# An attention-weight kernel of a recommender: the set-up stage reordered (loads, warm-up matmuls, biases, layout, split of the bank reads)

## Chip, cores and metric

The kernel runs on one core of a Trainium2 chip. The metric is the device time of one execution in microseconds, the median of several.

## The reference

For each of B = 2048 rows with one candidate vector `c` (32 numbers) and N = 200 goods vectors `g` (32 numbers each):

```python
outer = jnp.einsum('bi,bnj->bnij', candidate_ad, goods).reshape(Bs, Ns, Ks * Ks)
k_b = jnp.broadcast_to(candidate_ad[:, None, :], (Bs, Ns, Ks))
h1 = jnp.concatenate((k_b, goods, outer), axis=-1)
act = jax.nn.sigmoid(h1 @ W1 + b1)          # 36 hidden numbers
weight = act @ W2 + b2
out = jnp.sum(goods * weight, axis=1)
```

Because `outer` is a product of `c` and `g`, `h1 @ W1` is `g` times a 32x36 matrix that depends on the row alone (W1's goods part plus the outer part contracted with `c`), plus a bias that depends on the row alone (`c @ W1_cand + b1`). The kernel builds these per-row matrices and biases once and then streams the goods.

## The kernel before, in words

Four rows of B lie side by side on the 128 partitions (32 each) and make a unit; there are 512 units, and 8 units make a pair (64 pairs).

**Set-up.** The candidates (`cand`, 1 MB: 128 partitions of 8 KB), W1's outer part (`w1`, named `w_outer` in the trace) and small constants are loaded. In nine steps (`step(i)`, L229) TensorE makes, for four hidden numbers at a time, the outer part of the weights: one PSUM bank of 512 columns for each `x` in 0..3, from row group `x` of `cand` and of `w1`. Step 0 makes the last four hidden numbers (h = 32..35, the left-over weights), steps 1 to 8 the 32 main ones. Even steps write the four banks of `z_ps`, odd steps `x_ps`, `w_ps` and the two `s_ps`. Each bank is read out with W1's goods part added: ACT takes x = 0 and 2 (L350), DVE x = 1 and 3 (L377), 18 banks each. A step from 2 on waits for the reads of the step two before. The main banks go to `wm`. The left-over banks go to `wxd` with the four hidden numbers innermost, so that ACT and DVE write with a step of four elements (16 bytes). POOL first zeroes `wx` (L182) and then copies `wxd` into it (L189, `lay_out`, four copies of 32x256 elements for 8 pairs; `lay_out(0)` and `lay_out(1)` in the set-up, the six others in the loop, each behind the split of pair q = 0, 8, ... 40).

Between step 0 and step 1 TensorE makes the biases: L238 (32 columns of weights against 512 columns of `cand`, four column groups, all from row group 0) into `x_ps`, and L245 into `w_ps`. DVE reads both (L380, L383), and step 1 waits for these reads, since it writes the same banks.

**Main loop.** For each pair p, TensorE multiplies goods by `wm` (`products`, L265) and by `wx` (`products_x`, L281), ACT takes the sigmoid (L363, L359), TensorE sums over the hidden numbers (L301, `row_sums`), DVE keeps the sum (`whole`, L390), POOL splits it into three bf16 parts (L201 to L210, `top`, `rest`, `mid`, `stack`), TensorE spreads these over partitions (L317, `spread`, three pairs later), and DVE multiplies with the goods and sums (L398). SP issues the loads of the goods (L168) once `w1` and the constants have landed, into seven slots. `cand`, `candu` and `w1` lie in the memory that `act` takes later. The order on each queue is that of the program; semaphores tie the engines together. An f32 matmul is two records in the trace, so a bank of step 0 to 8 is 8 records.

Of the kernel before, what the change touches and what calls it, by code (L numbers as in the profile page):

```python
# [6 lines left out]
BF16 = mybir.dt.bfloat16  # L7
ALU = mybir.AluOpType
# [14 lines left out]
STORE = 16  # L23
WX_CHUNK = 8
WX_AHEAD = 2
RUN = 16
POOLED_ORDER = (0, 4, 2, 6)

# [14 lines left out]
def build(nc, goods_t, cand_r, cand_u, w1_outer, small, pick, out_t):  # L43
    with ExitStack() as ctx:
        def sb(name, shape, dt=F32):
            return ctx.enter_context(nc.sbuf_tensor(name, shape, dt))
# [6 lines left out]

        goods = sb("goods", [P, G_SLOTS, PAIR_U, N])
        wm = sb("wm", [P, UNITS // RUN, HM, RUN])
        wxd = sb("wxd", [P, UNITS // 2, 2, HX])
        warm = sb("warm", [P, 1])
        wx = sb("wx", [P, UNITS // 2, 3, 16])
        act = sb("act", [P, A_SLOTS, 4, 2 * N])
        actx = sb("actx", [P, A_SLOTS, N])  # L60
# [45 lines left out]

        def wxd_units(x):

            return wxd[:, :, :, x].rearrange("j (p c) s -> j p s c", c=4)

        def wb_units(x):
            return wb_bank(0, x).rearrange("j (p s c) -> j p s c", s=2, c=4)

        def wm_units(h):
            return wm[:, :, h, :]
# [5 lines left out]
        cand_loaded = sem("cand_loaded")  # L121
# [20 lines left out]

        block = ctx.enter_context(nc.Block())

        def kept(i, x):

            return 2 * i + x // 2 + 1

        KEPT_ALL = 2 * (T_MAIN + 1)

        def laid_out(k):

# [1 line left out]

        @block.sync
        def _(sp):
            sp.dma_start(cand[:, :, :], cand_r[:, :, :]).then_inc(cand_loaded, 16)
            sp.dma_start(candu[:, :], cand_u[:, :]).then_inc(candu_loaded, 16)

            sp.wait_ge(w1_loaded, 16)  # L160
            sp.wait_ge(consts_loaded, 16)
            for p in range(PAIRS):
                for j, v in enumerate(POOLED_ORDER):
                    if p >= G_SLOTS:

# [12 lines left out]
            sp.wait_ge(out_stored, 16 * (PAIRS // STORE))  # L178

        @block.gpsimd  # L180
        def _(pool):
            nc.gpsimd.memset(wx[:, :, :, :], 0.0).then_inc(wx_step, 1)  # L182

            def lay_out(k):

                of = slice(4 * WX_CHUNK * k, 4 * WX_CHUNK * (k + 1))
                for r in range(4):
                    rows = slice(32 * r, 32 * r + 32)
                    nc.gpsimd.tensor_copy(wx[rows, of, 0::2, HX * r:HX * r + HX], wxd[rows, of, :, :]).then_inc(wx_step, 1)  # L189
                    pool.wait_ge(wx_step, 4 * k + r + 2)  # L190

            pool.wait_ge(wx_step, 1)

            pool.wait_ge(wb_kept[0], kept(0, 2))
            pool.wait_ge(wb_kept[1], kept(0, 3))
            for k in range(WX_AHEAD):
                lay_out(k)
            pool.wait_ge(consts_loaded, 16)
            for q in range(PAIRS):
                pool.wait_ge(w_kept, q + 1)  # L200
                nc.gpsimd.tensor_scalar(top[:, :], whole[:, q % 2, :], m1, None, ALU.mult).then_inc(part_step, 1)  # L201
                pool.wait_ge(part_step, 4 * q + 1)
                nc.gpsimd.tensor_tensor(rest[:, :], whole[:, q % 2, :], top[:, :], ALU.subtract).then_inc(part_step, 1)  # L203
                pool.wait_ge(part_step, 4 * q + 2)
                nc.gpsimd.tensor_scalar(mid[:, :], rest[:, :], m2, None, ALU.mult).then_inc(part_step, 1)  # L205
                pool.wait_ge(part_step, 4 * q + 3)
                if q >= 2:

                    pool.wait_ge(s_done, 2 * (q - 1))
                nc.gpsimd.tensor_tensor(stack[:, q % 2, :], rest[:, :], mid[:, :], ALU.subtract).then_inc(part_step, 1)  # L210
                k = q // WX_CHUNK + WX_AHEAD
                if q % WX_CHUNK == 0 and k < PAIRS // WX_CHUNK:
                    pool.wait_ge(part_step, 4 * q + 4)
                    lay_out(k)

        @block.tensor
        def _(pe):
            pe.wait_ge(w1_loaded, 16)
            pe.wait_ge(cand_loaded, 16)

            def step(i):
                for x in range(4):
                    if i == 1 and x < 2:

                        pe.wait_ge(bias_kept, x + 1)
                    if i >= 2:
                        pe.wait_ge(wb_kept[x % 2], kept(i - 2, x))
                    for c in range(4):
                        last = nc.tensor.matmul(wb_bank(i, x)[32 * c:32 * c + 32, :],  # L229
                                                w1[32 * x:32 * x + 32, STEPS[i], :],  # L230
                                                cand[32 * x:32 * x + 32, c, :], start=True, stop=True)
# [39 lines left out]

            def products_x(p, s):
                if s == 0:
                    if p % WX_CHUNK == 0:
                        pe.wait_ge(wx_step, laid_out(p // WX_CHUNK))
                    if p >= 1:

                        pe.wait_ge(act_done, 4 * p)
                for c in range(4):
                    left = wx[:, 4 * p + c, s:s + 2, :].rearrange("p b m -> p (b m)")  # L280
                    last = nc.tensor.matmul(x_bank(p)[32 * c:32 * c + 32, 0:N], left,  # L281
                                            goods[:, p % G_SLOTS, 4 * s + c, :], start=s == 0, stop=s == 1)
                if s == 1:
                    last.then_inc(x_done, 1)
# [52 lines left out]
        def _(sc):  # L337
# [4 lines left out]
            sc.wait_ge(warm_set, 1)  # L342
            nc.scalar.activation(warm[:, :], warm[:, :], ACT.Sigmoid)
            sc.wait_ge(consts_loaded, 16)
            for i, t in enumerate(STEPS):
                for x in (0, 2):
                    sc.wait_ge(wb_made, 4 * i + x + 1)
                    h = 4 * t + x
                    out, src = (wxd_units(x), wb_units(x)) if i == 0 else (wm_units(h), wb_runs(i, x))
                    nc.scalar.activation(out, src, ACT.Identity, bias=w1g[:, h:h + 1]).then_inc(wb_kept[0], 1)  # L350
            sc.wait_ge(bias_kept, 2)
            for p in range(PAIRS):
                if p >= A_SLOTS:
# [14 lines left out]
        @block.vector  # L368
        def _(dve):
            nc.vector.memset(warm[:, :], 0.0).then_inc(warm_set, 1)  # L370
            dve.wait_ge(consts_loaded, 16)
            for i, t in enumerate(STEPS):
                for x in (1, 3):
                    dve.wait_ge(wb_made, 4 * i + x + 1)
                    h = 4 * t + x
                    out, src = (wxd_units(x), wb_units(x)) if i == 0 else (wm_units(h), wb_runs(i, x))
                    nc.vector.tensor_scalar(out, src, w1g[:, h:h + 1], None, ALU.add).then_inc(wb_kept[1], 1)  # L377
# [96 lines left out]
```

## Time and profile before

| | |
|---|---|
| Median of 3 runs | 292.26 us (291.7 to 293.32) |
| The profiled execution's own time | 290.82 us |
| Its span, first to last instruction | 289.0 us |
| Granted TensorE clock, mean | 0.984 of full speed |
| Busy: PE, DVE, ACT, POOL | 262.6, 193.2, 203.4, 195.8 us |

The set-up is everything up to the first goods matmul; the loop is what follows. A time line entry gives its start, its length, the engine, the line of the kernel, what is written and read, and how many records it merges.

### The profile page before, as it was taken

The page shows a single profiled execution, that of the slowest core. Times are in us where ns is not written, and L with a number is a line of the kernel's source. Part 1 is how long each engine was busy: PE and PEld are TensorE (multiplying, and loading weights), DVE is VectorE, ACT ScalarE, POOL GpSimd, SP SyncE. Part 2 cuts the span into 40 slices and gives each one's busy share as a digit, 9 for nine tenths or more (in the row PEclk, how much of TensorE's full clock was granted, in tenths as well). Part 3 has the DMA queues.
Part 4 walks back from the last instruction along what each step waited for, and adds up shares of the span by engine and source line. Part 5 has one row for each costly group of instructions (what it writes and reads, how often), then busy time and mean ns, then how long its engine had stood idle before and what let it go on. Part 6 is the DMA issues. An engine that isn't in the chain of part 4 may idle for free.

```text
span 289.0 us, 17645 instructions
## 1 busy us (share of the span) xinstructions
PE 262.6 (91%) x7480; PEld 159.9 (55%) x7480; DVE 193.2 (67%) x1109; ACT 203.4 (70%) x596; POOL 195.8 (68%) x293
## 2 busy tenths in 40 slices
PE   1997999999999999999999999999999999999931
PEld 0343665565665656656566656556556666666610
DVE  0593167776767767767677767766677767777775
ACT  2495878766787767886777877777877777787710
POOL 9900486668776777768667876678766666776671
PEclk9997999999999999999999999999999999999996
DMA  6895056776766767766777767777677777762000
GB/s 243 251 346 203 5 153 196 232 205 202 226 198 205 219 203 225 215 204 212 198 221 206 227 204 207 229 207 224 206 212 216 222 208 226 227 203 93 6 0 9
DMA packets 38238, 55.59 MB, mean 192 GB/s; under 512 B 4240, under 2 KB 37904, under 8 KB 38032
## 3 DMA queue, kind: packets, MB, share of 16 engines
q1 hardware_dynamic: 37728, 54.02, 61.8%
q8 instruction: 59, 0.97, 1.3%
q10 hardware_dynamic: 432, 0.45, 0.4%
q14 instruction: 19, 0.16, 0.2%
HBM read 54.19 MB, written 0.26 MB: 188 GB/s over the span
## 4 chain that ended last, share of the span: by engine, by line
PE 74%; POOL 10%; DVE 5%; issue 5%; ACT 3%; DMA 2%; POOLq 0%; DVEq 0%
PE z_ps L265 23%; PE w_ps L301 20%; PE s_ps L317 13%; PE x_ps L281 8%; PE z_ps L281 8%; DVE goods L398 4%; ACT wm L350 3%; POOL wx L189 2%; POOL mid L205 2%; POOL top L201 2%; DMA act<-w_outer 2%; POOL stack L210 2%; POOL rest L203 2%; PE x_ps L265 2%; PE z_ps L229 1%
## 5 line engine op out<-in xcount | busy, mean ns | idle before, releaser
L398 DVE CUSTOM_DVE_ANT_0 goods<-s_ps,goods 128x200 f32<-128x200 f32 x512 | 156.7, 362 | 73.2 <-PE s_ps L317 73.2
L363 ACT ACTIVATE act<-z_ps,bias 128x200 f32<-128x200 f32 x448 | 154.2, 440 | 62.5 <-PE z_ps L265 61.2
L201 POOL TENSOR_SCALAR top<-whole,consts 128x200 bf16<-128x200 f32 x64 | 50.1, 783 | 67.9 <-DVE whole L390 67.3
L265 PE MATMUL z_ps<-goods,wm 32*32 32x200 f32 x3584 | 87.7, 357 | 1.7 <-issue 1.6
L265 PEld LDWEIGHTS z_ps<-goods,wm 32*32 32x32 f32 x3584 | 57.0, 145 | 20.7 <-issue 14.2
L317 PE MATMUL s_ps<-stack,pick_sb 64*128 64x200 bf16 x512 | 44.7, 251 | 14.8 <-DVE out_stage L398 7.5
L301 PE MATMUL w_ps<-act,consts 128*32 128x200 f32 x1024 | 55.9, 333 | 0.0
L205 POOL TENSOR_SCALAR mid<-rest,consts 128x200 bf16<-128x200 f32 x64 | 50.1, 783 | 6.3
L317 PEld LDWEIGHTS s_ps<-stack,pick_sb 64*128 64x128 bf16 x512 | 16.4, 94 | 55.9 <-issue 43.9
L398 DVE DVE_READ_ACCUMULATOR2_ANT out_stage<- 128x1 f32 x512 | 42.6, 83 | 0.0
L203 POOL TENSOR_TENSOR rest<-whole,top 128x200 f32<-128x200 f32 x64 | 36.3, 567 | 5.3
L210 POOL TENSOR_TENSOR stack<-rest,mid 128x200 bf16<-128x200 f32 x64 | 36.2, 566 | 5.3
L301 PEld LDWEIGHTS w_ps<-act,consts 128*32 128x32 f32 x1024 | 33.8, 110 | 10.1 <-issue 0.2
L265 PE MATMUL x_ps<-goods,wm 32*32 32x200 f32 x512 | 37.7, 355 | 0.0
L301 PE MATMUL w_ps<-actx,consts 128*32 128x200 f32 x512 | 35.2, 333 | 0.1
L390 DVE TENSOR_SCALAR whole<-w_ps,consts 128x200 f32<-128x200 f32 x64 | 27.0, 421 | 10.2 <-PE w_ps L301 10.2
L281 PE MATMUL x_ps<-goods,wx 128*32 128x200 f32 x512 | 29.5, 345 | 0.0
L281 PE MATMUL z_ps<-goods,wx 128*32 128x200 f32 x512 | 28.8, 340 | 0.0
L363 ACT ACTIVATE act<-x_ps,bias 128x200 f32<-128x200 f32 x64 | 25.3, 475 | 0.0
L301 PEld LDWEIGHTS w_ps<-actx,consts 128*32 128x32 f32 x512 | 17.5, 110 | 5.7 <-issue 0.8
L281 PEld LDWEIGHTS x_ps<-goods,wx 128*32 128x32 f32 x512 | 13.6, 110 | 9.1 <-issue 6.2
L281 PEld LDWEIGHTS z_ps<-goods,wx 128*32 128x32 f32 x512 | 13.5, 108 | 8.1 <-issue 5.4
(34 smaller groups left out, 134.9 us busy)
## 6 DMA issues: line engine op xcount, KB each, us to landing
goods<-goods_t SPq DMA_DIRECT2D x256, 200.0 KB, 2.8
act<-cand_r SPq DMA_DIRECT2D x1, 1024.0 KB, 5.3
act<-cand_u SPq DMA_DIRECT2D x1, 256.0 KB, 6.0
out_t<-out_stage SPq DMA_DIRECT2D x4, 64.0 KB, 3.4
consts<-small ACTq DMA_DIRECT2D x1, 164.5 KB, 6.2
act<-w_outer ACTq DMA_DIRECT2D x1, 144.0 KB, 5.5
pick_sb<-pick ACTq DMA_DIRECT2D x1, 128.0 KB, 5.8
```

What stands on the lines that cost most here:

```text
L201: nc.gpsimd.tensor_scalar(top[:, :], whole[:, q % 2, :], m1, None, ALU.mult).then_inc(part_step, 1)
L203: nc.gpsimd.tensor_tensor(rest[:, :], whole[:, q % 2, :], top[:, :], ALU.subtract).then_inc(part_step, 1)
L205: nc.gpsimd.tensor_scalar(mid[:, :], rest[:, :], m2, None, ALU.mult).then_inc(part_step, 1)
L210: nc.gpsimd.tensor_tensor(stack[:, q % 2, :], rest[:, :], mid[:, :], ALU.subtract).then_inc(part_step, 1)
L265: last = nc.tensor.matmul(z_bank(p, r)[32 * c:32 * c + 32, N * s:N * s + N], wm[32 * r:32 * r + 32, u // RUN, :, u % RUN], goods[32 * r:32 ...
L281: last = nc.tensor.matmul(x_bank(p)[32 * c:32 * c + 32, 0:N], left, goods[:, p % G_SLOTS, 4 * s + c, :], start=s == 0, stop=s == 1)
L301: last = nc.tensor.matmul(w_ps[32 * t:32 * t + 32, 0:N], left, right, start=step == 0, stop=step == 2)
L317: last = nc.tensor.matmul(s_ps[s][:, N * i:N * i + N], pick_sb[rows, 2 * f + i, :], stack[rows, q % 2, :], start=True, stop=True)
L350: nc.scalar.activation(out, src, ACT.Identity, bias=w1g[:, h:h + 1]).then_inc(wb_kept[0], 1)
L363: last = nc.scalar.activation(act[:, p % A_SLOTS, r, N * s:N * s + N], z_bank(p, r)[:, N * s:N * s + N], ACT.Sigmoid, bias=bias[:, r, p, s ...
L390: nc.vector.tensor_scalar(whole[:, p % 2, :], w_ps[:, 0:N], b2, None, ALU.add).then_inc(w_kept, 1)
L398: last = nc.vector.tensor_tensor_reduce(goods[:, q % G_SLOTS, v, :], s_ps[s][:, N * i:N * i + N], goods[:, q % G_SLOTS, v, :], 1.0, 0.0, A ...
```

## The change

Six edits, all in the set-up, one of which reaches into the loop:

1. `cand` comes in four loads, one for each row group of 32 partitions, each with a semaphore of its own. Step 0 waits for load x ahead of bank x.
2. `warm` becomes a 128x512 bf16 tile of zeros, and TensorE multiplies it 8 times (512 columns each, into `s_ps[1]`) before it waits for `w1`. The small tile for ACT's table load is now `table`.
3. The biases are made after step 8 instead of after step 0, once the reads of step 7 are done. ACT reads the main bias (`x_ps`), after its banks; DVE reads `biasx`. `products_x(0, 0)` waits for both; ACT did before its first sigmoid and does still.
4. `wxd` has the hidden number outermost, and step 0 reads `cand` in the order (p, c, s), so ACT and DVE write the left-over banks with consecutive elements.
5. POOL's copies `wx <- wxd` read four hidden numbers that now lie 512 elements (2 KB) apart, for each of 64 consecutive positions. This holds for all 32 copies, also the 24 in the loop.
6. `OWNER` gives bank x = 1 of step 4 to ACT: ACT reads 19 banks, DVE 17.

```diff
+WARM = 8
+ACT_THREE = 4
-        wxd = sb("wxd", [P, UNITS // 2, 2, HX])
-        warm = sb("warm", [P, 1])
+        wxd = sb("wxd", [P, HX, UNITS // 2, 2])
+        warm = sb("warm", [P, BANK], BF16)
+        table = sb("table", [P, 1])
...
-            return wxd[:, :, :, x].rearrange("j (p c) s -> j p s c", c=4)
-
-        def wb_units(x):
-            return wb_bank(0, x).rearrange("j (p s c) -> j p s c", s=2, c=4)
+            return wxd[:, x, :, :].rearrange("j a s -> j (a s)")
...
+        OWNER = [[0, 0 if i == ACT_THREE else 1, 0, 1] for i in range(T_MAIN + 1)]
+
         def kept(i, x):
-            return 2 * i + x // 2 + 1
+            e = OWNER[i][x]
+            return sum(OWNER[j][y] == e for j in range(i + 1) for y in range(4) if j < i or y <= x)
...
-            sp.dma_start(cand[:, :, :], cand_r[:, :, :]).then_inc(cand_loaded, 16)
+            for x in range(4):
+                rows = slice(32 * x, 32 * x + 32)
+                sp.dma_start(cand[rows, :, :], cand_r[rows, :, :]).then_inc(cand_loaded[x], 16)
...
-                    nc.gpsimd.tensor_copy(wx[rows, of, 0::2, HX * r:HX * r + HX], wxd[rows, of, :, :]).then_inc(wx_step, 1)
+                    nc.gpsimd.tensor_copy(wx[rows, of, 0::2, HX * r:HX * r + HX],
+                                          wxd[rows, :, of, :].rearrange("p h j s -> p j s h")).then_inc(wx_step, 1)
...
+            pe.wait_ge(warm_set, 1)
+            for k in range(WARM):
+                nc.tensor.matmul(s_ps[1][:, :], warm[:, 0:P], warm[:, :], start=True, stop=True)
             pe.wait_ge(w1_loaded, 16)
-            pe.wait_ge(cand_loaded, 16)
 
             def step(i):
                 for x in range(4):
-                    if i == 1 and x < 2:
-
-                        pe.wait_ge(bias_kept, x + 1)
+                    if i == 0:
+                        pe.wait_ge(cand_loaded[x], 16)
                     if i >= 2:
-                        pe.wait_ge(wb_kept[x % 2], kept(i - 2, x))
+                        pe.wait_ge(wb_kept[OWNER[i - 2][x]], kept(i - 2, x))
                     for c in range(4):
+                        right = cand[32 * x:32 * x + 32, c, :]
+                        if i == 0:
+
+                            right = right.rearrange("i (p s c) -> i p c s", s=2, c=4)
...
-            step(0)
+            for i in range(T_MAIN + 1):
+                step(i)
+
+            pe.wait_ge(wb_kept[0], kept(T_MAIN - 1, 2))
+            pe.wait_ge(wb_kept[1], kept(T_MAIN - 1, 3))
             pe.wait_ge(consts_loaded, 16)
...
-            for i in range(1, T_MAIN + 1):
-                step(i)
-            pe.wait_ge(wb_kept[0], KEPT_ALL)
-            pe.wait_ge(wb_kept[1], KEPT_ALL)
+            pe.wait_ge(wb_kept[0], kept(T_MAIN, 2))
+            pe.wait_ge(wb_kept[1], kept(T_MAIN, 3))
...
+                    if p == 0:
+
+                        pe.wait_ge(bias_kept, 2)
...
+            sc.wait_ge(bias_made, 1)
+            nc.scalar.activation(bias[:, :, :, :].rearrange("p r q s -> p (r q s)"), x_ps[:, :], ACT.Identity,
+                                 bias=b1m).then_inc(bias_kept, 1)
             sc.wait_ge(bias_kept, 2)
...
-                if i == 0:
-                    dve.wait_ge(bias_made, 1)
-                    nc.vector.tensor_scalar(bias[:, :, :, :].rearrange("p r q s -> p (r q s)"), x_ps[:, :], b1m,
-                                            None, ALU.add).then_inc(bias_kept, 1)
-                    dve.wait_ge(bias_made, 2)
-                    nc.vector.tensor_scalar(biasx[:, :], w_ps[:, 0:PAIRS], b1x, None, ALU.add).then_inc(bias_kept, 1)
+            dve.wait_ge(bias_made, 2)
+            nc.vector.tensor_scalar(biasx[:, :], w_ps[:, 0:PAIRS], b1x, None, ALU.add).then_inc(bias_kept, 1)
```

## Rows read from the trace of the kernel before

**Rows 1.** The page: busy times, then the chain's shares by line

```profile
PE 262.6 (91%) x7480; PEld 159.9 (55%) x7480; DVE 193.2 (67%) x1109; ACT 203.4 (70%) x596; POOL 195.8 (68%) x293
...
PE z_ps L265 23%; PE w_ps L301 20%; PE s_ps L317 13%; PE x_ps L281 8%; PE z_ps L281 8%; DVE goods L398 4%; ACT wm L350 3%; POOL wx L189 2%; POOL mid L205 2%; POOL top L201 2%; DMA act<-w_outer 2%; POOL stack L210 2%; POOL rest L203 2%; PE x_ps L265 2%; PE z_ps L229 1%
```

**Rows 2.** Time line of the set-up, 0 to 27 us (start, length, idle time before)

```profile
0.71 10.34 POOL L182 MEMSET wx<- 128x12288 f32 x1 [0.29 <-POOLq L463]
0.72 0.38 SPq L157 DMA_DIRECT2D act<-cand_r  x1
...
6.23 2.02 PE L229 MATMUL z_ps<-act 32*32 32x512 f32 x32 [6.23 <-DMA act<-w_outer]
...
7.94 2.25 PE L238 MATMUL x_ps<-act,consts 32*32 32x512 f32 x8
...
8.29 2.23 ACT L350 ACTIVATE wxd<-z_ps,consts 128x512 f32<-128x512 f32 x2 [4.68 <-PE z_ps L229]
8.40 2.18 DVE L377 TENSOR_SCALAR wxd<-z_ps,consts 128x512 f32<-128x512 f32 x2 [7.55 <-PE z_ps L229]
...
10.12 0.68 PE L245 MATMUL w_ps<-act,consts 128*32 128x64 f32 x16
...
13.37 0.75 DVE L377 TENSOR_SCALAR wm<-w_ps,consts 128x512 f32<-128x512 f32 x1 [2.05 <-PE s_ps L229]
...
18.82 0.63 PE L229 MATMUL x_ps<-act 32*32 32x512 f32 x4
...
19.27 0.61 PE L229 MATMUL x_ps<-act 32*32 32x512 f32 x4
...
22.60 1.40 DVE L377 TENSOR_SCALAR wm<-z_ps,consts 128x512 f32<-128x512 f32 x2
...
24.10 2.01 PE L265 MATMUL z_ps<-goods,wm 32*32 32x200 f32 x64 [1.62 <-issue]
...
26.01 2.02 ACT L363 ACTIVATE act<-z_ps,bias 128x200 f32<-128x200 f32 x6 [3.34 <-PE z_ps L265]
```

**Rows 3.** The chain in order of time, ACT's part of the set-up

```profile
14.47 8.21 ACT wm L350 x14
```

**Rows 4.** The page: DMA issues, KB each, microseconds from issue to landing

```profile
act<-cand_r SPq DMA_DIRECT2D x1, 1024.0 KB, 5.3
...
consts<-small ACTq DMA_DIRECT2D x1, 164.5 KB, 6.2
act<-w_outer ACTq DMA_DIRECT2D x1, 144.0 KB, 5.5
```

**Rows 5.** Busy time by stretch: us, engines, granted clock (PEclk), DMA share, GB/s

```profile
23.00:24.00 1.00, 0.00 (x0) 0.00 (x0) 1.00 (x2) 0.00 (x0) 0.00 (x0) 0.94 1.05 389
24.00:25.00 1.00, 0.90 (x34) 0.70 (x35) 0.00 (x0) 0.00 (x0) 0.00 (x0) 0.50 1.00 375
```

**Rows 6.** The writers and readers of `wxd` (ns: min/median/max), and ACT's plain bank reads

```profile
L189 POOL COPY wx<-wxd x32: 386/393/405, 11.1 to 195.2; 32x256 f32<-32x256 f32 x32
L350 ACT ACTIVATE wxd<-z_ps,consts x2: 1193/1228/1262, 8.3 to 9.3; 128x512 f32<-128x512 f32 x2
L377 DVE TENSOR_SCALAR wxd<-z_ps,consts x2: 1129/1172/1215, 8.4 to 9.4; 128x512 f32<-128x512 f32 x2
...
L350 ACT ACTIVATE wm<-s_ps,consts 128x512 f32<-128x512 f32 x4 | 2.9, 718 | 0.0
```

**Rows 7.** Time line of the loop around one lay-out, 60 to 75 us

```profile
62.20 1.37 PE L265 MATMUL z_ps<-goods,wm 32*32 32x200 f32 x64
...
63.48 2.02 ACT L363 ACTIVATE act<-z_ps,bias 128x200 f32<-128x200 f32 x6 [1.29 <-PE z_ps L265]
...
67.01 1.75 POOL L189 COPY wx<-wxd 32x256 f32<-32x256 f32 x4
...
71.26 0.57 POOL L210 TENSOR_TENSOR stack<-rest,mid 128x200 bf16<-128x200 f32 x1
...
71.97 0.35 PE L317 MATMUL s_ps<-stack,pick_sb 64*128 64x200 bf16 x4
```

More of the change, by code:

```diff
@@ L120, in build @@
         consts_loaded = sem("consts_loaded")
-        cand_loaded = sem("cand_loaded")
+        cand_loaded = [sem(f"cand_loaded{x}") for x in range(4)]
         candu_loaded = sem("candu_loaded")
@@ L143, in build @@
         block = ctx.enter_context(nc.Block())
+        OWNER = [[0, 0 if i == ACT_THREE else 1, 0, 1] for i in range(T_MAIN + 1)]
         def kept(i, x):
-            return 2 * i + x // 2 + 1
-        KEPT_ALL = 2 * (T_MAIN + 1)
+            e = OWNER[i][x]
+            return sum(OWNER[j][y] == e for j in range(i + 1) for y in range(4) if j < i or y <= x)
         def laid_out(k):
@@ L217, in _ @@
         def _(pe):
+            pe.wait_ge(warm_set, 1)
+            for k in range(WARM):
+                nc.tensor.matmul(s_ps[1][:, :], warm[:, 0:P], warm[:, :], start=True, stop=True)
             pe.wait_ge(w1_loaded, 16)
-            pe.wait_ge(cand_loaded, 16)
             def step(i):
                 for x in range(4):
-                    if i == 1 and x < 2:
-                        pe.wait_ge(bias_kept, x + 1)
+                    if i == 0:
+                        pe.wait_ge(cand_loaded[x], 16)
                     if i >= 2:
-                        pe.wait_ge(wb_kept[x % 2], kept(i - 2, x))
+                        pe.wait_ge(wb_kept[OWNER[i - 2][x]], kept(i - 2, x))
                     for c in range(4):
+                        right = cand[32 * x:32 * x + 32, c, :]
+                        if i == 0:
+                            right = right.rearrange("i (p s c) -> i p c s", s=2, c=4)
                         last = nc.tensor.matmul(wb_bank(i, x)[32 * c:32 * c + 32, :],
-                                                w1[32 * x:32 * x + 32, STEPS[i], :],
-                                                cand[32 * x:32 * x + 32, c, :], start=True, stop=True)
+                                                w1[32 * x:32 * x + 32, STEPS[i], :], right, start=True, stop=True)
                     last.then_inc(wb_made, 1)
-            step(0)
+            for i in range(T_MAIN + 1):
+                step(i)
+            pe.wait_ge(wb_kept[0], kept(T_MAIN - 1, 2))
+            pe.wait_ge(wb_kept[1], kept(T_MAIN - 1, 3))
             pe.wait_ge(consts_loaded, 16)
@@ L340, in _ @@
             sc.dma_start(pick_sb[:, :, :], pick[:, :, :]).then_inc(pick_loaded, 16)
-            sc.wait_ge(warm_set, 1)
-            nc.scalar.activation(warm[:, :], warm[:, :], ACT.Sigmoid)
+            sc.wait_ge(warm_set, 2)
+            nc.scalar.activation(table[:, :], table[:, :], ACT.Sigmoid)
             sc.wait_ge(consts_loaded, 16)
             for i, t in enumerate(STEPS):
[L346 to L350, printed above, removed]
+                for x in range(4):
+                    if OWNER[i][x] == 0:
+                        sc.wait_ge(wb_made, 4 * i + x + 1)
+                        h = 4 * t + x
+                        out, src = (wxd_units(x), wb_bank(0, x)) if i == 0 else (wm_units(h), wb_runs(i, x))
+                        nc.scalar.activation(out, src, ACT.Identity, bias=w1g[:, h:h + 1]).then_inc(wb_kept[0], 1)
+            sc.wait_ge(bias_made, 1)
+            nc.scalar.activation(bias[:, :, :, :].rearrange("p r q s -> p (r q s)"), x_ps[:, :], ACT.Identity,
+                                 bias=b1m).then_inc(bias_kept, 1)
             sc.wait_ge(bias_kept, 2)
@@ L370, in _ @@
             nc.vector.memset(warm[:, :], 0.0).then_inc(warm_set, 1)
+            nc.vector.memset(table[:, :], 0.0).then_inc(warm_set, 1)
             dve.wait_ge(consts_loaded, 16)
             for i, t in enumerate(STEPS):
[L373 to L377, printed above, removed]
-                if i == 0:
-                    dve.wait_ge(bias_made, 1)
-                    nc.vector.tensor_scalar(bias[:, :, :, :].rearrange("p r q s -> p (r q s)"), x_ps[:, :], b1m,
-                                            None, ALU.add).then_inc(bias_kept, 1)
-                    dve.wait_ge(bias_made, 2)
-                    nc.vector.tensor_scalar(biasx[:, :], w_ps[:, 0:PAIRS], b1x, None, ALU.add).then_inc(bias_kept, 1)
+                for x in range(4):
+                    if OWNER[i][x] == 1:
+                        dve.wait_ge(wb_made, 4 * i + x + 1)
+                        h = 4 * t + x
+                        out, src = (wxd_units(x), wb_bank(0, x)) if i == 0 else (wm_units(h), wb_runs(i, x))
+                        nc.vector.tensor_scalar(out, src, w1g[:, h:h + 1], None, ALU.add).then_inc(wb_kept[1], 1)
+            dve.wait_ge(bias_made, 2)
+            nc.vector.tensor_scalar(biasx[:, :], w_ps[:, 0:PAIRS], b1x, None, ALU.add).then_inc(bias_kept, 1)
             def keep(p):
```

## The prediction

> **What bounds it now.** I read the page first, then the time line of the set-up, then the loop around one lay-out. The page [rows 1] says that TensorE is busy 91% of the span and that the chain runs mostly through its loop lines; the loop can only be moved by something on that chain. In the set-up the chain runs otherwise [rows 2, 3]: the matmuls start at 6.23 when `w1` lands, both readers start at 8.3 to 8.4, and from 13.37 DVE reads 16 banks without a gap, to 22.60 + 1.40 = 24.00. That is 10.63 / 16 = 0.664 us a bank. ACT does 14 banks in 8.21 us, 0.586 each, and is done 1.3 us earlier. So the set-up ends when DVE ends, and the first goods matmul follows at 24.10. Before 13.37 DVE has done little: two left-over banks, the biases, and then 2.05 us of waiting for step 1, which stood behind the biases. That hole, the biases in front of it and DVE's tail are what the change aims at.
>
> Two more things are to be seen. The granted clock falls just before 24 us and is 0.50 in the next microsecond [rows 5]: the first goods matmuls run at 1.2 GHz after TensorE has idled for 1.6 us. And POOL's lay-out in the loop is on the chain (L189, 2% of the span [rows 1]): in the one shown, four copies take 1.75 us, the next `stack` ends late, at 71.83, and the spread that needs it starts at 71.97 [rows 7]. There are six of these in the loop, and what is added to a copy is added to the time nearly in full.
>
> **The parts.**
>
> *Loads.* SP's issue took 0.38 us [rows 2], so the fourth load is issued at about 0.72 + 3 x 0.43 = 2.0. The bytes are the same, so it lands no earlier than the one load did, 0.72 + 5.3 = 6.0; the set-up's loads took 5.3 to 6.2 us from issue [rows 4], which gives at latest 2.0 + 6.2 = 8.2. No load to 32 partitions is in this trace. I take 8.2, since the separate issues are real and each small load needed over 5 us in this crowd. `candu` is issued 1.3 us later and is wanted only by the biases, now 10 us later; it costs nothing. The goods' loads wait for `w1` and the constants, which the order on ACT's queue leaves where they were (7.4); they have ten microseconds in hand.
>
> The Trainium skill, in SBUF — State Buffer, the section on the DMA port swizzle, says that a transfer to partitions 0 to 31 reaches only half of the DMA ports; by that the four loads would run at about half the rate, and the fourth would land late rather than early. No run shows it yet.
>
> *Zeros.* DVE's larger memset is bounded by POOL's wx memset, 10.34 us for 12288 elements: 512 take 0.43 at most, so TensorE starts at about 1.2. A f32 record of 512 columns takes 0.61 at the higher clock [rows 2]; the 8 bf16 matmuls are between 0.3 and 1.1 each (the step-0 block took 2.02 for two rounds at the lower clock), and I take half a f32 record of the low clock, 0.5, so they end near 5.3, ahead of `w1`. If they took 1.1 they would end at 10 and hold up step 0; I give that little. What they buy is the clock at step 0.
>
> *Step 0 and the start of DVE's run.* Bank 3 of step 0 starts with its load, 8.2. A bank alone at the higher clock took 18.82 to 19.88, 1.06 us [rows 2]; at the lower one L238, the same shape, took 2.25. I take the higher: DVE's unbroken run of 16 banks (bank 3 of step 0 and the 15 later ones that it keeps) starts at 9.3 instead of 13.37. Bank 1 of step 0 lies before that. The reads of `cand` with a step in step 0 are priced by L238, which has such reads too and whose records are like the others': nothing. The left-over writes without a step are 0.4 to 0.5 us shorter each [rows 6], but lie ahead of 9.3 and are covered. So DVE ends at 9.3 + 10.63 = 19.9 to 20.0: **-4.0 us**. ACT has 17 banks after step 0, 17 x 0.586 = 10.0 from about 9.5, so it ends at 19.5: the moved bank evens the two out; without it DVE would end 0.66 later.
>
> *Biases at the end.* They may start when step 7 has been read; DVE's last two banks begin at its end less 1.40. Low clock: 2.25 + 0.68 = 2.9 us [rows 2], so 1.5 past DVE's end. High clock: about half, 1.5 in all, so 0.1 to 0.4 past. The first goods matmul stands behind them on TensorE's queue: **+0.3** (low clock: +1.4). ACT's bias read (0.72, like a bank) is behind that first bank of products by half a microsecond or more, as is biasx: hidden by products(0), 1.3 us long, and `products_x(0, 0)`, which now waits for them, comes after it.
>
> *The clock in the first products.* Before, the first sigmoid started 26.01 - 24.10 = 1.91 after the first goods matmul; in the loop it is 63.48 - 62.20 = 1.28 [rows 7]. With the biases in the gap, TensorE no longer idles for 1.6 us ahead of them: **-0.6**, and nothing if the clock falls all the same. ACT then sets the pace of the first pairs, so there is no more to gain.
>
> *POOL's copies.* In the set-up, the copies start after the memset, at 11.1, and are wanted at about 21.7: covered even at double the time. In the loop, 24 copies of 0.393 us. The lower bound of what the new read costs is 0: the destination was scattered before and is the same, and a contiguous read cannot become cheaper by being scattered. The upper: a step of 16 bytes cost DVE 1.172 - 0.75 = 0.42 us and ACT 1.228 - 0.718 = 0.51 us per 512 elements [rows 2, 6], so 0.21 to 0.26 per copy; as a share of ACT's time, 71%, 0.28 per copy. That is 5.1 to 6.7 us over 24. Those rows are writes, on other engines; the row nearest is the copy itself, which already writes in runs of four at 1.5 ns an element, nearly twice the memset's 0.84. I take 0.
>
> The sum: -4.0 + 0.3 - 0.6 = **-4.3 us**, so a span of 284.7 and a time of 286.5 against the profiled execution's 290.82. That execution is 1.4 under the median; on the median the forecast is 292.26 - 4.3 = **288.0**.
>
> **Rivals.**
>
> *A: the copies pay for the step, and it eats the gain.* At DVE's price, 0.21 x 24 = +5.1, net +0.8: 293.1, no change to be told. For it: the chain does run through L189, and the only rows with a step show a price. Against: those are writes, into memory whose consecutive elements were 16 bytes apart. 27%.
>
> The Trainium skill, GPSIMD Engine Reference, section on performance pitfalls for Q7 kernels, speaks for it: reads of SBUF with a step over 8 bytes cost half as much again per element. By that page alone a copy would be 0.59 us, the loop 4.7 us longer and the time 292.7 (an estimate).
>
> *B: slower.* The same place at a higher price: the copies at +0.28 (6.7 us) with a set-up that gains only 3: net +3.7, 296.0. It decides from +0.24 us a copy on with the gain of 4.3 (24 x 0.24 = 5.8, 1.46 above the gain). 12%.
>
> *C: the clock is not there.* The zeros end about a microsecond before `w1` lands; in the set-up's end 1.6 us of idling came before the fall. Then bank 3 is ready at 8.2 + 2.25 = 10.4, two steps are made at 1.7 to 2 us instead of 1.3 (-0.8), and the end of the set-up may be at the low clock too: gain 4.3 - 1.1 - 0.8 - 0.6 = 1.8, time 290.5. That the zeros do nothing is this rival as well. 12%.
>
> *D: everything early.* The fourth load lands at 6.0; then the constants (1.16 + 6.2 = 7.36) let the readers go, and 17 x 0.664 ends at 18.7: gain 5.3 + 0.3 = 5.6, time 286.7. 7%.
>
> The forecast itself has 42%; its own range is 286.5 to 289.8.
>
> **How the numbers follow.** A measurement can tell 0.5%, 1.46 us, from no change: faster is under 290.8, slower over 293.7. Faster: forecast 0.41, D 0.07, half of C 0.06, a fifth of A 0.06: 0.60. Same: half of C, half of A and a little: 0.23. Slower: a quarter of A, B: 0.17. The range 286.0 to 293.8 leaves out B and the edges.
>
> **What would show it.** In the changed trace: DVE's bank reads without a gap from 9 to 10 us, ending at 20; L189 copies still at 0.39 (right) or 0.6 (A); L317 waits for `stack` of the same length; L238 after step 8, and a granted clock of 1.00 in the first goods matmuls. The forecast is wrong if the copies are longer than 0.45, if bank 3 of step 0 is read later than 10.5, or if the first goods matmul comes over 0.8 after DVE's last bank.

## The result, and the profile after

The changed kernel takes 300.85 us (median of 4 runs, 299.25 to 302.78) against 292.67 us before (4 runs, 291.7 to 293.32): ratio 1.030, 95% interval 1.0255 to 1.0347. It is slower by 3%; the forecast was 288.0, with a range to 293.8. The profiled execution took 302.78, its span is 301.0. It is the slowest of the four, and the profiled one of before (290.82) was quicker than its median, so the two traces lie 12 us apart where the medians lie 8. Ratios, here and below, leave out executions over 1.5% above the fastest of their kernel; medians are of all.

The page of the changed kernel: busy times, the chain's shares by line, and POOL's copies (count, then busy us, mean ns, idle before):

```profile
PE 273.3 (91%) x7488; PEld 162.9 (54%) x7488; DVE 191.8 (64%) x1108; ACT 205.7 (68%) x598; POOL 203.4 (68%) x293
...
PE z_ps L277 19%; PE w_ps L316 18%; PE s_ps L332 11%; PE x_ps L296 8%; PE z_ps L296 7%; POOL wx L193 5%; DVE goods L415 4%; POOL top L206 3%; POOL mid L210 3%; POOL stack L215 2%; POOL rest L208 2%; ACT wm L366 2%; DMA act<-cand_r 2%; PE z_ps L240 2%; PE x_ps L277 2%
...
L193 POOL COPY wx<-wxd 32x256 f32<-32x256 f32 x32 | 20.3, 636 | 3.3 <-ACT wm L366 1.4
```

A copy takes 0.636 us where it took 0.393 [rows 6], and its line has 5% of the chain instead of 2% [rows 1]. POOL as a whole is busy no larger share of the span than before (68%): the average does not show it, the chain does.

Where the 12 us lie can be read from the times at which DVE keeps the sums (`whole`, L390 before, L407 after), one a pair, 3.88 us apart in an undisturbed pair. The first comes at 32.94 instead of 31.47: the set-up lost 1.5 us. The last comes 11.9 us later than before. The 10.4 us in the loop come from the pairs behind the six lay-outs, 3 after each q = 0, 8, ... 40. With the excess over 3.88 in brackets: pair 3 (1.1), pairs 10 and 11 (1.4), 19 (1.4), 27 (3.0), 35 (2.8), 43 (3.0), 12.7 in all. Everything else in the loop that exceeds 3.88 adds up to 1.5 us after; before, all excess together is 3.8, of which 0.7 lies at pairs 3, 27 and 35. The time line of the changed kernel around the fourth lay-out, POOL, DVE and TensorE:

```profile
136.97 0.64 POOL L193 COPY wx<-wxd 32x256 f32<-32x256 f32 x1
137.70 0.78 POOL L206 TENSOR_SCALAR top<-whole,consts 128x200 bf16<-128x200 f32 x1
139.13 0.42 DVE L407 TENSOR_SCALAR whole<-w_ps,consts 128x200 f32<-128x200 f32 x1
140.10 0.56 POOL L215 TENSOR_TENSOR stack<-rest,mid 128x200 bf16<-128x200 f32 x1
140.72 0.35 PE L332 MATMUL s_ps<-stack,pick_sb 64*128 64x200 bf16 x4 [1.47 <-POOL stack L215]
141.00 1.56 PE L296 MATMUL x_ps<-goods,wx 128*32 128x200 f32 x16
146.03 0.42 DVE L407 TENSOR_SCALAR whole<-w_ps,consts 128x200 f32<-128x200 f32 x1
```

TensorE stands 1.47 us until `stack` is there, and then `products_x` takes 1.56 us instead of the 0.9 of other pairs. What changed is seen in the busy time by stretch (us, PE, PEld, DVE, ACT, POOL, granted clock, DMA share, GB/s):

```profile
140.00:141.00 1.00, 0.28 (x5) 0.12 (x5) 0.00 (x0) 1.00 (x4) 0.92 (x3) 1.00 0.85 216
141.00:141.50 0.50, 0.50 (x10) 0.37 (x12) 0.39 (x3) 0.17 (x1) 0.42 (x1) 0.54 0.72 256
...
142.00:143.00 1.00, 1.00 (x17) 0.62 (x13) 0.34 (x4) 0.38 (x2) 0.85 (x2) 0.50 0.30 55
```

The clock falls from 2.4 to 1.2 GHz right behind the wait and stays there to 144.5. It does so at the fourth, fifth and sixth lay-out (pairs 27, 35, 43), which cost 2.8 to 3.0 us, and not at the first three, which cost 1.1 to 1.4. The six waits for `stack` are 1.20, 0.88, 1.53, 1.47, 1.25 and 1.54 us: the third had no fall and the shorter fifth had one, so the length of the wait alone does not decide it.

The set-up of the changed kernel, from its time line (first the zeros, then step 0 and what followed):

```profile
1.17 3.53 PE L226 MATMUL s_ps<-warm 128*128 128x512 bf16 x8 [1.17 <-DVE table L390]
5.23 2.15 PE L240 MATMUL z_ps<-act 32*32 32x512 f32 x16 [0.53 <-DMA act<-w_outer]
7.76 2.80 PE L240 MATMUL z_ps<-act 32*32 32x512 f32 x12 [0.39 <-DMA act<-cand_r]
9.52 1.08 PE L240 MATMUL x_ps<-act 32*32 32x512 f32 x4
11.48 0.75 DVE L398 TENSOR_SCALAR wxd<-z_ps,consts 128x512 f32<-128x512 f32 x1 [3.21 <-PE w_ps L240]
15.13 0.75 DVE L398 TENSOR_SCALAR wm<-z_ps,consts 128x512 f32<-128x512 f32 x1 [0.31 <-PE x_ps L240]
21.76 1.40 DVE L398 TENSOR_SCALAR wm<-z_ps,consts 128x512 f32<-128x512 f32 x2
21.94 1.98 PE L252 MATMUL x_ps<-act,consts 32*32 32x512 f32 x8 [0.26 <-ACT wm L366]
24.44 1.70 PE L277 MATMUL z_ps<-goods,wm 32*32 32x200 f32 x64
```

Its clock and DMA by stretch, and for comparison two microseconds of the kernel before's load in the fence behind:

```profile
6.00:7.00 1.00, 1.00 (x12) 0.15 (x8) 0.00 (x0) 0.36 (x1) 1.00 (x1) 1.00 1.08 242
7.00:8.00 1.00, 0.61 (x8) 0.15 (x8) 0.48 (x1) 0.33 (x1) 1.00 (x1) 0.96 0.90 209
8.00:9.00 1.00, 1.00 (x8) 0.00 (x0) 0.27 (x1) 0.00 (x0) 1.00 (x1) 0.50 1.00 272
...
30.00:31.00 1.00, 1.00 (x15) 0.54 (x16) 0.00 (x0) 1.00 (x4) 0.00 (x0) 0.50 0.06 16
```

```profile
4.00:5.00 1.00, 0.00 (x0) 0.00 (x0) 0.00 (x0) 0.00 (x0) 1.00 (x1) 1.00 1.01 419
5.00:6.00 1.00, 0.00 (x0) 0.00 (x0) 0.00 (x0) 0.00 (x0) 1.00 (x1) 1.00 0.98 373
```

Three things are to be seen. The zeros did speed up step 0: the records of its first two banks, from 5.23, took 0.70 to 0.72 us, where all of step 0 before took 1.06. (The granted clock cannot show this. In the kernel before its column has 1.00 for step 0 as well, although the records are as long as those of 9.5 to 11 us in the changed kernel, where it has 0.50. For the start of the program go by the length of a record.) But the loads for the row groups came one after the other, the last shortly before 9.5, at 209 to 272 GB/s instead of 373 to 419; TensorE stood between them, the granted clock fell just before 8 and was low until 14.75, and bank 3 was read at 11.48. So DVE's reads had gaps until 15.13 and ended at 21.76 + 1.40 = 23.16, not at 20. And the biases (L252) took 1.98 us at the high clock, so that the first goods matmul came 1.28 us behind DVE's last bank, at 24.44 [rows 2: 24.10]. After them the clock fell again and stayed low from 25.0 to 31.8, twice as long as before (23.9 to 27.3).

### The profile page after: what moved, and what is told of

Same layout as the page of the kernel before. It is cut to its first block, busy times and chain, and to the rows that moved or that the text cites. A ratio compares the mean times of both kernels' runs of the same rounds, so it can differ in the third digit from the quotient of the medians.

```text
span 301.0 us, 17667 instructions
## 1 busy us (share of the span) xinstructions
PE 273.3 (91%) x7488; PEld 162.9 (54%) x7488; DVE 191.8 (64%) x1108; ACT 205.7 (68%) x598; POOL 203.4 (68%) x293
## 4 chain that ended last, share of the span: by engine, by line
PE 69%; POOL 16%; DVE 5%; issue 5%; ACT 2%; DMA 2%; SPq 0%; POOLq 0%; DVEq 0%
PE z_ps L277 19%; PE w_ps L316 18%; PE s_ps L332 11%; PE x_ps L296 8%; PE z_ps L296 7%; POOL wx L193 5%; DVE goods L415 4%; POOL top L206 3%; POOL mid L210 3%; POOL stack L215 2%; POOL rest L208 2%; ACT wm L366 2%; DMA act<-cand_r 2%; PE z_ps L240 2%; PE x_ps L277 2%
## 5 line engine op out<-in xcount | busy, mean ns | idle before, releaser
L316 PE MATMUL w_ps<-act,consts 128*32 128x200 f32 x1024 | 57.6, 343 | 0.0
L316 PEld LDWEIGHTS w_ps<-act,consts 128*32 128x32 f32 x1024 | 34.7, 113 | 11.2 <-DVE whole L407 0.2
L407 DVE TENSOR_SCALAR whole<-w_ps,consts 128x200 f32<-128x200 f32 x64 | 27.0, 422 | 10.8 <-PE w_ps L316 10.8
L296 PE MATMUL x_ps<-goods,wx 128*32 128x200 f32 x512 | 31.1, 363 | 0.0
L193 POOL COPY wx<-wxd 32x256 f32<-32x256 f32 x32 | 20.3, 636 | 3.3 <-ACT wm L366 1.4
```

The source lines that it names most:

```text
L316: last = nc.tensor.matmul(w_ps[32 * t:32 * t + 32, 0:N], left, right, start=step == 0, stop=step == 2)
L407: nc.vector.tensor_scalar(whole[:, p % 2, :], w_ps[:, 0:N], b2, None, ALU.add).then_inc(w_kept, 1)
```

## The experiments

The kernels ran in three groups of four (1 to 4; 6, 7, 8 and the first run of 9; the rest), each group on one chip beside the kernel before. There the kernel before spread from 291.0 to 301.9 us. The traces show stalls of TensorE's queue of 0.3 to 1.7 us at changing places of the loop, which the profile puts down to "issue"; that these make the spread is likely and not shown, since no trace of a long execution of the kernel before was kept. The small ratios have wide intervals, and I read the mechanisms from the traces.

**1. The new layout alone**, on the kernel before (edits 4 and 5):

```diff
-        wxd = sb("wxd", [P, UNITS // 2, 2, HX])
+        wxd = sb("wxd", [P, HX, UNITS // 2, 2])
...
+                    nc.gpsimd.tensor_copy(wx[rows, of, 0::2, HX * r:HX * r + HX],
+                                          wxd[rows, :, of, :].rearrange("p h j s -> p j s h")).then_inc(wx_step, 1)
```

Expected: 

> The kernel before with edits 4 and 5 alone (hidden number outermost in wxd, step 0 in the order p, c, s, copies that read with a step). Theory 1, the copies: the six lay-outs of the loop get 1 us longer each and TensorE's wait for stack brings the clock down in some of them, so 8 to 11 us over before, some 301 to 303; copies at 0.64 us. Theory 2, the set-up's new order is what costs: within 1 us of before.

Measured: 301.91 us against 295.26, ratio 1.021 (1.012 to 1.030). The copies' row in the view of `wxd` (ns: min/median/max) and TensorE's waits for `stack` (us in total, times, longest):

```profile
L189 POOL COPY wx<-wxd x32: 602/634/659, 11.1 to 201.8; 32x256 f32<-32x256 f32 x32
```

```profile
PEld s_ps L320 <- POOL stack L211: 14.1, 9, 1.9
PE s_ps L320 <- POOL stack L211: 7.1, 6, 1.5
```

The kernel before has 8.2 and 0.8 us in these two. The last `whole` of the trace comes 7.9 us later than before's, with the first at 31.49, as before. The copies alone do it. In this execution the clock fell at none of the six lay-outs, although three of the waits for `stack` were 1.52 us, as long as in the changed kernel (the others 1.19, 0.67 and 0.64); the lay-outs cost 1.1 to 1.4 us each. It is the fastest of the four, 298.81 us at a mean granted clock of 0.983. The other three took 301.73 to 303.45 at 0.965 to 0.967, which is 10 to 11 us more at the low clock, about three falls of 3.4 us (an estimate; they have no trace). So the same waits seem to bring the clock down in some executions and not in others, as expected; the 8 to 11 us over before were not reached (6.7 between the medians).

**2. The set-up's edits without the new layout**: the changed kernel with edits 4 and 5 undone.

```diff
-        wxd = sb("wxd", [P, HX, UNITS // 2, 2])
+        wxd = sb("wxd", [P, UNITS // 2, 2, HX])
...
-                        if i == 0:
-                            right = right.rearrange("i (p s c) -> i p c s", s=2, c=4)
```

Expected: 

> The changed kernel with edits 4 and 5 undone; loads, zeros, biases last and the split of the banks stay. Theory 1: the loop runs as before, and only the 1.5 us that the set-up lost stay, less what is noise: 292.5 to 295; copies at 0.39 us. Theory 2: 299 or more.

Measured: ratio 0.992 (0.986 to 0.999), median 296.51 against 295.26 with both widely spread, copies 0.393 us, first `whole` at 30.79. The ratio rests on three of the ten executions, and the median of all ten is no better than before's: the times show neither a gain nor a loss. The trace shows a first `whole` 0.7 us earlier than before, not 1.5 later as in the changed kernel, so the expected "1.5 us that the set-up lost" were not there. Two things differ. With the new layout step 0 reads `cand` with a step, and its first records took 0.70 to 0.72 us where here most took 0.59 to 0.60; and the clock was low for 6.8 us from 8 on where here it was for 3.4. The changed kernel's second low stretch, from 25.0, was also twice as long as here. In the traces of experiments 3 and 4, with the new layout, the first `whole` comes at 32.34 and 31.11, so part of the 1.5 changes from execution to execution. What made the change slow is the layout.

**3. One copy a pair**: the changed kernel, with each lay-out of the loop spread over four pairs.

```diff
-                for r in range(4):
+                for r in rs:
...
-                if q % WX_CHUNK == 0 and k < PAIRS // WX_CHUNK:
+                if q % WX_CHUNK < 4 and k < PAIRS // WX_CHUNK:
                     pool.wait_ge(part_step, 4 * q + 4)
-                    lay_out(k)
+                    lay_out(k, [q % WX_CHUNK])
```

Expected: 

> The changed kernel, each lay-out of the loop spread over four pairs, one copy behind each. POOL idled 0.92 us a pair, and one copy with its wait takes 0.70. Theory 1 (what counts is whether stack comes late): no wait for stack over 0.5 us, no fall of the clock between 40 and 280 us, copies still 0.64 us, and 10 us less than the changed kernel: 290 to 293. Rival (the longer copies cost by POOL's total busy time or by contention for memory): still over 297.

Measured: 294.84 us against 295.26, ratio 1.001 (0.995 to 1.007). The changed kernel's ratio was 1.030, on another chip; on this one, experiment 4, which keeps the lumps of four, took 301.61. The copies are still long, and the waits on TensorE itself are gone (the weight loads' 6.2 us left lie in the first pairs and at the end):

```profile
L193 POOL COPY wx<-wxd x32: 603/620/657, 13.4 to 210.1; 32x256 f32<-32x256 f32 x32
```

```profile
PEld s_ps L332 <- POOL stack L215: 6.2, 6, 1.6
```

No pair behind a lay-out is longer than 3.89 for q = 0, 8 and 16; behind the other three, four pairs are 0.1 to 0.7 us longer, with no wait of a matmul for `stack`. The clock doesn't fall in the loop. So the 0.24 us a copy cost nothing that can be told where POOL's idle 0.9 us a pair covers them: what counted was that four stood ahead of one `stack`. In microseconds it is 2 above the 290 to 293 expected, as the kernel before is on this chip.

**4. The step on the other side**: the changed kernel, the copies read 64 consecutive elements and write with the step.

```diff
-                    nc.gpsimd.tensor_copy(wx[rows, of, 0::2, HX * r:HX * r + HX],
-                                          wxd[rows, :, of, :].rearrange("p h j s -> p j s h")).then_inc(wx_step, 1)
+                    nc.gpsimd.tensor_copy(wx[rows, of, 0::2, HX * r:HX * r + HX].rearrange("p j s h -> p h j s"),
+                                          wxd[rows, :, of, :]).then_inc(wx_step, 1)
```

Expected: 

> The changed kernel, the copies' loops turned: 64 consecutive elements of wxd are read for each hidden number, and the step (64 bytes and more) is in the writes to wx. If the step of the read is what costs: 0.39 to 0.45 us a copy and 291 to 294. If a step on either side costs the same: 0.6 us or more and no gain.

Measured: 301.61 us, ratio 1.021 (1.012 to 1.030), no gain on the new layout (301.91 in experiment 1), and

```profile
L193 POOL COPY wx<-wxd x32: 601/634/720, 11.9 to 205.1; 32x256 f32<-32x256 f32 x32
```

A step on the write side costs the same as one on the read side. Only with consecutive elements in the inner run on both sides (four, as before) is it 0.393 us. It is not the read alone that costs. In this trace the clock fell at the third, fourth and fifth lay-out, behind waits of 1.59 to 1.60 us; the other three waits, 0.97 to 1.28, had none.

**5. Double the suspected cost**: the kernel before, each copy of the loop made twice (the result is the same).

```diff
-                    nc.gpsimd.tensor_copy(wx[rows, of, 0::2, HX * r:HX * r + HX], wxd[rows, of, :, :]).then_inc(wx_step, 1)
-                    pool.wait_ge(wx_step, 4 * k + r + 2)
+                    for again in range(2 if k >= WX_AHEAD else 1):
+                        nc.gpsimd.tensor_copy(wx[rows, of, 0::2, HX * r:HX * r + HX], wxd[rows, of, :, :]).then_inc(wx_step, 1)
+                        made[0] += 1
+                        pool.wait_ge(wx_step, made[0])
```

Expected: 

> The kernel before, each of the 24 copies of the loop made twice over (same result): a lay-out takes 3.6 us instead of 1.8, 1.75 more, where the changed layout's took 0.96 more. Theory: every pair with a lay-out is 1.8 to 2.3 us longer than 3.88, so 11 to 13 us in all, and TensorE's wait for stack, now over 2 us, brings the clock down to 1.2 GHz in four or more of the six, with 1.5 us more for each: 305 to 312 us. Rival (the clock's falls in the changed kernel were chance, without a tie to the wait): no more than one fall in the loop, 302 to 305.

Measured in a single execution: 309.55 us against 294.65. Pairs 3 and 11 are 1.93 us longer than 3.88, without a fall; pairs 19, 27, 35 and 43 are 3.4 to 4.2 us longer, each with a fall of the clock behind a wait of 1.93 to 2.36 us. At the third:

```profile
110.51 0.44 PE L321 MATMUL s_ps<-stack,pick_sb 64*128 64x200 bf16 x4 [2.36 <-POOL stack L214]
110.88 1.56 PE L285 MATMUL x_ps<-goods,wx 128*32 128x200 f32 x16
```

This bears out both parts of the price of a lay-out: what it is too long goes to the pair in full, and a fall of the clock adds 1.4 to 2.3 us. Falls came at 0, 3 and 3 of six waits of 0.6 to 1.6 us (experiments 1 and 4 and the changed kernel) and at four of six waits of 1.9 to 2.4. The two without a fall were 2.05 and 2.06 us long and one with a fall 1.93: longer waits have more falls, and what decides a single one stays open. The kernel before, whose longest wait for `stack` in the loop is 0.55, has none.

**6 to 8. The set-up's parts**, all with the old layout. *Biases last alone*: one load, no zeros, 18 banks each. *One load*: the set-up's edits with the load of `cand` in one. *No zeros*: the set-up's edits, four loads, without zeros.

```diff
-            for x in range(4):
-                rows = slice(32 * x, 32 * x + 32)
-                sp.dma_start(cand[rows, :, :], cand_r[rows, :, :]).then_inc(cand_loaded[x], 16)
+            sp.dma_start(cand[:, :, :], cand_r[:, :, :]).then_inc(cand_loaded[0], 16)
```

```diff
-WARM = 8
+WARM = 0
```

Expected of biases last alone: 

> The kernel before with edit 3 alone (biases after step 8): one load, no zeros, old layout, 18 banks each. Step 1 follows step 0, so the 2.05 us hole goes; but the biases cost 2.0 to 2.3 us at either clock, since at the higher clock L252 still took 1.98. Theory: DVE's last bank ends at about 22.2 (24.0 before), the first goods matmul at 23.5, the first whole at 30.5 to 31.5; the whole time 1 us less to equal. Rival (moving the biases is what lost the set-up's gain): the first goods matmul at 24.5 or later.

Expected of one load: 

> The set-up edits with the old layout and one load of cand again; zeros, biases last and 19/17 banks stay. Theory (the four loads of 32 partitions land one after the other, the last at 9 us, so that TensorE stands still between them and the clock falls at 8): step 0 runs as one block from 6.2, all its banks are there by 8.3, no fall of the clock at 8, DVE's last bank at 20.5 to 21.5, first whole at 28.5 to 30. Rival (the loads are harmless, 1.2 GHz comes anyway): within 0.5 us of the same kernel with four loads, first whole at 30.8.

Expected of no zeros: 

> The set-up edits with the old layout, four loads, and without the matmuls of zeros. If the zeros bring anything: step 0 at 1.2 GHz from its start and bank 3 of it later by up to 1 us than in the same kernel with zeros, first whole at 31.3 to 32. If they bring nothing, since the clock falls at 8 anyway: within 0.3 us of 30.8.

Measured, with the times that count, us:

| | step 0 from | first goods matmul | clock low from 20 to 32 | first `whole` | ratio to before |
|---|---|---|---|---|---|
| before | 6.23 | 24.10 | 23.9 to 27.3 | 31.47 | |
| biases last alone | 6.21 | 22.24 | no | 29.20 | 0.994 (0.989 to 0.999) |
| four loads, no zeros | 4.63 | 23.73 | 24.1 to 27.5 | 30.92 | 0.998 (0.992 to 1.005) |
| four loads, zeros (2) | 4.92 | 23.42 | 22.6 to 26.0 | 30.79 | 0.992 (0.986 to 0.999) |
| one load, zeros | 6.26 | 21.59 | no | 28.39 | 0.995 (0.990 to 0.999) |

Each row is one trace, except for the ratios, and the ratios tell no row from another. Biases last is worth 2.3 us at the first `whole`, more than I had expected: DVE's last bank ends at 20.96 and not at 22.2, and the clock didn't fall behind the biases in that execution. With one load step 0 is one block, DVE's last bank ends 1.8 us earlier than with four (20.31 against 22.11), and the first `whole` comes 2.4 us earlier, the rest being a fall of the clock that only the latter has; the two rows with four loads are 1.6 to 1.7 us behind biases last alone. So the four loads take back most of what the biases bring. With four loads the zeros are worth 0.1 us: the third bank's records take 0.59 us with them, the wait for load 3 follows, and the fourth's take 1.06. With one load they brought nothing in this trace either: step 0 took 2.02 us, as before, 1.5 us after the zeros had ended. In the four traces of 9 to 12, 1.5 to 1.9 us after them, its records took 0.6. The length of that gap does not tell the two apart.

**9 to 12. A version that beats both**: one load, zeros, biases last, 19 and 17 banks, the old layout, and one copy a pair (the diffs of 2, 3 and 6). It ran twice; beside it the second time ran one with 18 banks each (`ACT_THREE = -1`), and one in which the units of `cand` and `wm` are ordered by c first:

```diff
-                src = cand[0:K, :, :].rearrange("i r (p s c) -> i c r p s", s=2, c=4)
+                src = cand[0:K, :, :].rearrange("i r (c p s) -> i c r p s", s=2, c=4)
...
-                            u = PAIR_U * p + 4 * s + c
+                            u = 2 * PAIRS * c + 2 * p + s
```

Expected of the candidate: 

> A version to beat both: one load, zeros, biases last, 19/17 banks, the old layout, and each lay-out of the loop spread over four pairs. Theory: first whole at 28.5 to 30, no wait for stack over 0.3 us in the loop, 2 to 3.5 us under the kernel before: ratio 0.988 to 0.993. Rival (the set-up is bound elsewhere): ratio 0.997 to 1.003.

Expected of its second run: 

> The candidate once more, beside the version ordered by c: ratio to the kernel before 0.984 to 0.993 as before, and 0.2 to 0.4% over the version ordered by c.

Expected with 18 banks each: 

> The candidate with 18 banks each instead of 19 and 17. Theory: DVE ends one bank, 0.66 us, later; but the biases stand between it and the goods, so the first goods matmul comes only 0 to 0.7 us later and the first whole 0 to 0.7 us. If the biases are what the set-up's end waits for, nearer 0.6, since they start with the reads of step 7, which come 0.66 later as well.

Expected with c first: 

> The candidate, with the units in cand (and so in wm) ordered by c first, so that the bias matmuls L249 read 128 consecutive numbers at a time instead of every fourth. Theory (the step of 16 bytes held those matmuls at 1.07 us a record and 1.98 in all, though the clock was 2.4 GHz): 0.6 us a record, 1.1 to 1.3 in all, first whole 0.7 to 0.9 us earlier than in the candidate at the same clock. If the matmuls are bound by using one row group alone: 1.98 again and no gain.

Measured: the candidate 290.65 us against 295.44, ratio 0.989 (0.982 to 0.996), and the second time 291.28 against 294.65, ratio 0.981 (0.976 to 0.985), lower than expected and from three of its six executions; c first 291.08 beside it, 0.988 (0.984 to 0.991). Both beat the kernel before by 1 to 2%, and the lead of 0.2 to 0.4% that c first was to have does not show in the times. In the trace the set-ups can be told apart: first `whole` at 27.57 and 28.18 in the candidate's two executions (without and with a fall of the clock at 21), 28.59 with 18 banks each (with a fall, so 0.4 us for the moved bank, between the bounds expected), 27.09 with c first, although its clock was low from 7.3 to 10.7. That is 0.5 us before the candidate without a fall, where 0.7 to 0.9 at the same clock were expected. The bias matmuls, candidate and c first, both at the high clock:

```profile
18.22 1.98 PE L249 MATMUL x_ps<-act,consts 32*32 32x512 f32 x8 [0.15 <-ACT wm L363]
```

```profile
18.79 1.06 PE L249 MATMUL x_ps<-act,consts 32*32 32x512 f32 x8
```

The length of one record (ns: min/median/max) in the candidate, with c first, and of the same matmuls in the kernel before:

```profile
L249 PE MATMUL x_ps<-act,consts x8: 1058/1066/1074, 18.3 to 19.2; 32*32 32x512 f32 x8
```

```profile
L249 PE MATMUL x_ps<-act,consts x8: 587/600/612, 18.8 to 19.3; 32*32 32x512 f32 x8
```

```profile
L238 PE MATMUL x_ps<-act,consts x8: 1073/1076/1082, 7.9 to 9.1; 32*32 32x512 f32 x8
```

The step of 16 bytes in what they read held them at 1.98 us; reading consecutive numbers they take 1.06, the time of a bank of step 1 to 8. The rival, that the use of one row group alone bounds them, is out.

## Why the prediction was wrong

- **What bounds it: right.** The page's chain had L189 on it, and DVE's run of 16 banks ended the set-up.
- **"POOL's copies ... I take 0": the step that failed.** I had both bounds, 0 and 0.28 us a copy, and chose the lower with the argument that the copy already wrote in short runs. The row shows 0.636 - 0.393 = 0.243 us, near the upper. The argument was wrong in kind: the runs of four on the write side were consecutive, and their end is what costs little; an inner run with a step costs, whichever side it is on (experiment 4). The Trainium skill's rule (GPSIMD Engine Reference, performance pitfalls for Q7 kernels), half as much again per element for reads with a step over 8 bytes, pointed the right way and was too low. Measured here are 0.243 / 0.393 = 62%, and writes with a step cost the same.
- **"What is added to a copy is added to the time nearly in full": too low, and I had the row for it.** 0.97 us more a lay-out cost 1.0 to 1.4 us a pair where the clock held. Where the clock fell to 1.2 GHz behind TensorE's wait, it cost 2.8 to 3.0. I had costed the clock's fall in the set-up and never asked which other wait could grow long enough for one. With 24 x 0.243 = 5.8 in place of its 6.7, my own rival B would have ended at 292.26 + 2.8 = 295.1; the falls in the loop and a set-up that gained nothing make the rest.
- **The set-up's -4.3: it failed too.** It lost 1.5 us at the first `whole`, and gained 0.7 with the old layout (experiment 2). So with free copies as well the kernel would have stayed near the old time and not at 288.0. The parts follow.
- **Loads: 8.2 taken, about 9.4 measured** (the four landings took 3.7 to 7.4 us from issue). The upper bound of 2.0 + 6.2 was not one: the rows were of loads to 128 partitions. The rate fell to 209 to 272 GB/s from 373 to 419. The Trainium skill's rule of the DMA port swizzle (SBUF — State Buffer), half the ports for a load to 32 partitions, would give half of 373 to 419, 187 to 210 (an estimate; `w1` and the constants ran beside them to all partitions). The trace agrees roughly; no run separates the ports from another cause.
- **Zeros: right in length** (3.53 us, done at 4.70, against 5.3 forecast), and step 0's first records were shorter for them. The gain was lost as rival C said, here with the waits for the loads. That the gap ahead of `w1` can lose it as well, the trace with one load (7) suggests.
- **Start of DVE's run: 9.3 taken, bank 3 read at 11.48**, in pieces until 15.13. This is rival C's 10.4 and two slow steps, and a microsecond more.
- **Biases: +0.3 taken, 1.28 measured.** I halved L238's time for the clock. It hardly changed with the pace (2.25 in the kernel before, behind a step 0 with records of 1.06; 1.98 at a granted 1.00 in the changed one), since its reads had a step; I had even costed such reads at nothing, from a row at the low pace, where the step is hidden (1.076 a record against 1.056). The c-first kernel shows it.
- **Clock in the first products: -0.6 taken.** It fell behind the biases and stayed low for 6.8 us. In the eleven traces with biases last it fell within the biases or the first products behind them in seven and held in four. The biases filled the time and did not always hold the clock. All five traces with four loads are among the seven, and two of the six with one load, among them one of the candidate's two: the loads may bear on it and do not settle it. TensorE was without a gap from L252 on in both kinds.
- **The left-over writes: right** (0.69 and 0.75 us), and covered. The split of the banks: right in size, at most 0.4 us at the first `whole`.

Of the 11.9 us between the two traces' last `whole`, 1.5 are the set-up, 12.7 the pairs behind the lay-outs, and -2.3 the difference between their other stalls and all of before's. Most of that last part is luck of these two executions, for the stalls change places and number from trace to trace.

## What to carry to other kernels

When a layout is turned around so that its writer runs faster, count its readers: here four writes got 0.5 us shorter once, in cover, and 24 copies on a critical chain got 0.24 us longer each. Where a helper engine has slack of 0.9 us in every round, give it its extra work in pieces of that size; copies of the same length cost 7 us in lumps of four (301.61 against 294.84) and nothing that could be told singly. And price a wait on TensorE with the clock: here a late `stack` cost 1.0 to 1.4 us where the clock held, and up to 3.1 where it fell.

## What had not been expected of the hardware

- POOL's copy of 32x256 f32 takes 0.393 us with inner runs of four consecutive elements on both sides, and 0.634 with a step on the read side or on the write side alike.
- A matmul that reads f32 with a step of 16 bytes took 1.066 us a record of 512 columns at the granted 2.4 GHz, where the same one took 0.60 reading consecutive elements. In the kernel before, where consecutive reads took 1.056, it took 1.076.
- Behind TensorE's waits of 0.6 to 1.6 us in the loop the clock fell at three of six places in each of two kernels and at none in a third; behind waits of 1.9 to 2.4 us at four of six. The shortest wait with a fall was 1.25 us, the longest without 2.06. It then stayed at 1.2 GHz for 3.4 us or twice that. A stall put down to "issue" did it too (1.68 us at 119.5 in the c-first kernel), and one of the same length did not (experiment 3, at 125.0).
- The granted clock shows 1.00 at the start of the program while records have the length of the low level (1.06 us against 0.60).
- Stalls put down to "issue", 0.3 to 1.7 us, come at changing places: in the candidate's two traces, 297.61 and 292.75 us, the loops differ by 5.3 us. Their cause stays open.
